# A new issue order on four engines, and one square read from PSUM, in the recurrent stage of a decoder

## The reference

```
h    = layer_norm(x) * ln1_w;  prev = h shifted by one token
k    = (h * mix_k + prev * (1 - mix_k)) @ Wk        # v and r likewise; r goes through a sigmoid
scan over t:  out_t   = (e1 * num + e2 * v) / (e1 * den + e2)   # running maximum kept in mx
              num,den = e1' * num + e2' * v , e1' * den + e2'
x    = x + (r * out) @ Wo
h    = layer_norm(x) * ln2_w;  prev = h shifted by one token
kk   = (h * cmix_k + prev * (1 - cmix_k)) @ Wck      # 128 -> 512 features
vv   = square(relu(kk)) @ Wcv                        # 512 -> 128
rr   = sigmoid((h * cmix_r + prev * (1 - cmix_r)) @ Wcr)
x    = x + rr * vv
```

## Time and profile before

| | |
|---|---|
| median of 3 runs | 4856.62 us |
| the profiled execution, its span | 4856.43 us, 4854.6 us |
| the recurrent stage in the span | first DMA issue at 1861.12, last instruction ends at 3038.0 |
| PE / DVE / ACT / POOL busy over the span | 90% / 73% / 65% / 38% |
| mean granted TensorE clock over the span | 0.963 of full speed |

### The profile page before, as it was taken

How to read it: one execution, slowest core, us unless ns; L and a number is a source line. 1 busy time by engine, 2 the same in 40 slices (tenths; PEclk the granted TensorE clock), 3 DMA queues, 4 the chain that set the end, 5 groups by cost and what they waited for, 6 DMA issues and landing times. The chain is left out here.

```text
span 4854.6 us, 101446 instructions
## 1 busy us (share of the span) xinstructions
PE 4353.9 (90%) x37343; PEld 2843.6 (59%) x37343; DVE 3537.1 (73%) x5307; ACT 3133.0 (65%) x5627; POOL 1846.5 (38%) x2204
## 2 busy tenths in 40 slices
PE   8989788889979987999999999779979989999888
PEld 6767556657757763333333333566657767777665
DVE  7978777567763338999999996663349966666748
ACT  6878677567764346888888888663247854444356
POOL 4444345014407751333333331037734422222327
PEclk9999899899989998999999999889999999999999
DMA  3000000000021122000000000411130000000110
GB/s 105 2 2 3 2 1 1 1 13 3 3 65 53 52 79 67 1 1 1 1 1 0 1 0 1 120 35 53 52 106 3 3 1 2 2 2 1 56 55 36
DMA packets 123884, 119.28 MB, mean 25 GB/s; under 512 B 19472, under 2 KB 103952, under 8 KB 122640
## 3 DMA queue, kind: packets, MB, share of 16 engines
q1 hardware_dynamic: 106000, 77.11, 5.1%
q0 software_dynamic: 17408, 35.69, 2.6%
HBM read 82.34 MB, written 30.41 MB: 23 GB/s over the span
## 5 line engine op out<-in xcount | busy, mean ns | idle before, releaser
L1759 POOL DMA_INDIRECT L_ffn_xg<-L_ffn_xrows,L_ffn_take x272 | 263.2, 968 | 280.6 <-DVE L_ffn_take L2054 198.4
L1823 PEld LDWEIGHTS L_ffn_ps<-L_ffn_early_down,L_ffn_mT 128*128 128x128 f32 x1904 | 248.3, 191 | 105.1 <-issue 78.0
L1765 POOL DMA_INDIRECT L_ffn_yrows<-L_ffn_yo,L_ffn_put x272 | 268.3, 987 | 100.4 <-issue 57.0
L2944 POOL TENSOR_TENSOR L_xattn_E<-L_xattn_E,L_xattn_rz 128x1024 f32<-128x1024 f32 x64 | 123.8, 1934 | 471.2 <-DVE L_xattn_rz L3164 471.2
L2247 PE MATMUL L_attn_ps<-L_attn_mix,L_attn_wck 128*128 128x512 f32 x512 | 246.3, 603 | 50.4 <-DVE L_attn_xw L2640 50.4
L2452 POOL TENSOR_TENSOR L_attn_dn<-L_attn_ex,L_attn_den 128x504 f32<-128x504 f32 x64 | 80.9, 1264 | 519.3 <-issue 424.7
L1803 PE MATMUL L_ffn_ps<-L_ffn_up,L_ffn_xT 128*128 x544 | 258.6, 557 | 18.9 <-DVE L_ffn_xT L2091 7.6
L1823 PE MATMUL L_ffn_ps<-L_ffn_early_down,L_ffn_mT 128*128 x1904 | 259.5, 276 | 2.5 <-DVE L_ffn_yo L2084 1.3
L2262 PE MATMUL L_attn_ps<-L_attn_rl,L_attn_wcv 128*128 128x512 f32 x512 | 246.3, 604 | 6.7
L1913 ACT ACTIVATE L_ffn_mT<-L_ffn_ps 128x512 f32<-128x512 f32 x136 | 81.2, 597 | 236.6 <-PE L_ffn_ps L1812 236.6
L2398 ACT ACTIVATE L_attn_rl<-L_attn_ps 128x1024 f32<-128x1024 f32 x128 | 129.8, 1014 | 160.5 <-PE L_attn_ps L2247 160.5
(11 more groups left out here) (619 smaller groups left out, 13458.1 us busy)
## 6 DMA issues: line engine op xcount, KB each, us to landing
L_ffn_row_hot<-L_ffn_yrows SPq DMA_DIRECT2D x32, 256.0 KB, 3.0
L_ffn_col_hot<-L_ffn_yrows SPq DMA_DIRECT2D x32, 256.0 KB, 3.4
L_ffn_w<-in_L_ffn_e_W SPq DMA_DIRECT2D x32, 256.0 KB, 4.3
L_ffn_xrows<-L_ffn_xtok SPq DMA_DIRECT2D x42, 192.0 KB, 2.1
L_ffn_xg<-L_ffn_xrows,L_ffn_take POOLq DMA_INDIRECT x272, 2.5
L_ffn_yrows<-L_ffn_yo,L_ffn_put POOLq DMA_INDIRECT x272, 2.3
main_x<-in_xT SPq DMA_DIRECT2D x8, 512.0 KB, 8.0
main_ctx<-in_ctxT SPq DMA_DIRECT2D x4, 1024.0 KB, 11.5
```

The costliest lines, as they stand in the source:

```text
L1759: pool.indirect_dma_start(xg[t % RING][:], None, xrows, bass.IndirectOffsetOnAxis(ap=take[:, t:t + 1], axis=0)) \
L1765: pool.indirect_dma_start(yrows, bass.IndirectOffsetOnAxis(ap=put[:, t:t + 1], axis=0), yo[t % RING][:], None).then_inc(scattered[t % RING ...
L1823: g = pe.matmul(ps[1][:, 3, 0:P], mT[u][0:rows[a], a * P:(a + 1) * P], down[a][:, bass.ds(at, P)], start=(a == 0), stop=(a == FT - 1))
```

## The change

The second half's square takes one operand from another place: `rl * rl`, both from SBUF, becomes `rl * kk`, the rectified value times the value still in PSUM (the product is the same number, since the rectified value is either that value or zero). PSUM banks 5 and 6 are therefore read until that product is done, and `hidden(m, 0)` of the next turn, which writes them, waits for it (`srb`). All four engines get a new order, by new places; VectorE's `prepare` steps get one too. No instruction is added or removed.

```diff
                 elif m:
                     pe.wait_ge(xc3, m)
+                    pe.wait_ge(srb, m)
...
 # TensorE
-                            (1.7, variance1), (22.9, keys), (24.9, values), (30.2, receptance), (45.7, output),
-                            (50.5, variance2), (60.6, lambda m: hidden(m, 0)), (59.9, receptance2),
-                            (63.9, lambda m: hidden(m, 1)), (69.8, lambda m: contract(m, 0)),
-                            (71.3, lambda m: contract(m, 1)), (76.0, centred))),
-                        (TURNS, NT, END, END_PERIOD, ((5.1, variance1), (16.3, end_sum), (21.4, end_variance2))))
+                            (1.6, variance1), (24.4, keys), (26.8, values), (32.6, receptance), (45.5, output),
+                            (50.4, variance2), (62.5, lambda m: hidden(m, 0)), (60.3, receptance2),
+                            (66.3, lambda m: hidden(m, 1)), (71.1, lambda m: contract(m, 0)),
+                            (71.2, lambda m: contract(m, 1)), (77.2, centred))),
+                        (TURNS, NT, END, END_PERIOD, ((6.3, variance1), (17.8, end_sum), (21.5, end_variance2))))
...
 # ScalarE
-                            (-12.9, square1), (13.0, half_mixed_r), (8.4, half_mixed_k), (-4.3, rstd1), (28.2, exp_r), (29.6, ln_r),
-                            (28.0, ln_denominator), (19.4, exp_ab), (21.0, exp_g), (34.5, reciprocal),
-                            (39.0, square2), (42.3, rstd2), (47.0, half_mixed), (46.9, half_mixed_r2), (53.5, lambda m: rectified(m, 0)), (55.0, squared),
-                            (57.0, lambda m: rectified(m, 1)),
-                            (55.4, exp_rr), (58.0, ln_rr), (63.6, sigmoid_rr))),
-                        (TURNS, NT, END, END_PERIOD, ((-9.3, square1), (-0.1, rstd1), (8.6, end_square2), (15.7, end_rstd2))))
+                            (-24.4, square1), (10.7, half_mixed_r), (6.6, half_mixed_k), (-3.5, rstd1), (25.7, exp_r), (27.4, ln_r),
+                            (28.2, ln_denominator), (17.3, exp_ab), (17.0, exp_g), (31.8, reciprocal),
+                            (37.2, square2), (40.3, rstd2), (44.3, half_mixed), (42.7, half_mixed_r2), (52.3, lambda m: rectified(m, 0)), (55.6, squared),
+                            (55.8, lambda m: rectified(m, 1)),
+                            (57.0, exp_rr), (59.6, ln_rr), (60.1, sigmoid_rr))),
+                        (TURNS, NT, END, END_PERIOD, ((-10.7, square1), (-1.6, rstd1), (7.8, end_square2), (13.2, end_rstd2))))
...
 # GpSimd
-            staggered(TURNS, PERIOD, (13.8, denominator), (20.8, denominator_r), (26.5, quotient), (36.1, normal2))
+            staggered(TURNS, PERIOD, (17.6, denominator), (21.7, denominator_r), (32.9, quotient), (38.8, normal2))
...
 # VectorE
-                dve.tensor_tensor(rl[:, 2:4, :], rl[:, 2:4, :], rl[:, 2:4, :], ALU.mult).then_inc(srb, 1)
+                dve.tensor_tensor(rl[:, 2:4, :], rl[:, 2:4, :], ps[:, 5:7, :], ALU.mult).then_inc(srb, 1)
...
-                            (8.8, normal1), (23.1, mix_r), (18.7, mix_key), (34.7, clamp_r), (23.4, running_max), (26.3, exponents_ab),
-                            (26.4, exponent_g), (27.1, clamp_g), (28.7, weighted), (28.0, scan_den), (34.2, scan_num),
-                            (29.2, bonus), (34.9, numerator), (45.5, residual1), (57.9, mix_k), (56.8, mix_r2), (68.0, squared),
-                            (61.1, clamp_rr),
-                            (70.9, gated), (76.6, residual2))),
-                        (1, NL - 1, PERIOD, PERIOD, ((2.7, prepare),)),
-                        (TURNS, NT, END, END_PERIOD, ((10.9, normal1), (28.1, end_close))))
+                            (13.0, normal1), (21.7, mix_r), (14.9, mix_key), (31.4, clamp_r), (21.4, running_max), (24.1, exponents_ab),
+                            (22.4, exponent_g), (22.8, clamp_g), (29.2, weighted), (29.2, scan_den), (29.3, scan_num),
+                            (31.1, bonus), (32.0, numerator), (46.5, residual1), (53.1, mix_k), (51.3, mix_r2), (65.6, squared), 
+                            (63.2, clamp_rr),
+                            (68.4, gated), (72.4, residual2))),
+                        (1, NL - 1, PERIOD, PERIOD, ((-16.9, prepare),)),
+                        (TURNS, NT, END, END_PERIOD, ((9.8, normal1), (26.1, end_close))))
```

## The result

The changed kernel takes 4739.27 us (median of 4 runs, 4733.29 to 4746.61) against 4855.57 us for the kernel before on the same chip: a ratio of 0.9762, 95% interval 0.9745 to 0.9779, 116.3 us less. The forecast was 4738 us. The profiled execution took 4733.29 us (span 4731.5), 6 us under its own median.

The account below looks back on a forecast made before the run. VectorE, never resting, was taken as the bound: 17.16 us a turn less 2.40, plus 0.26, 0.12 and 0.06, gives 15.20. Over 62 turns 121.5 us less, 3 lost at the ends: 118.5 less, 4738 us, range 4708 to 4798.

Parts of the forecast that it names:

- The mechanism: GpSimd's four instructions each need about 1.07 us in which VectorE runs no instruction with two SBUF operands; first starter wins.
- One sign: GpSimd's `denominator` and `normal2` were to become longer than before, held by a scan and by `normal1`.
- `clamp_g` shut out: VectorE's `clamp_g` would be shut out by GpSimd's `quotient`, adding 0.26 us a turn (bounds 0 and 0.4).
- `clamp_g` behind its own input: VectorE's `clamp_g` directly behind `exponent_g`: 0.77 us start to start against 0.65 back to back, adding 0.12 a turn.
- The two handovers: `denominator` against `normal1` and `normal2` against `numerator` have no slack: 0.06 us a turn added (bounds 0 and 0.3).
- The new wait and the PSUM operand: TensorE's `hidden(m, 0)` waiting on the square costs nothing; the square from PSUM takes 1.22 us, gaining 0.16 a turn.
- TensorE next: TensorE's 34 matmuls a turn at 0.43 us make 14.6 us; no order goes below about 14.9 a turn.
- The ends: First and last turns: `prepare(1)` waiting for weights and a later `normal1(1)`, partly returned; 3 us lost (4 gained to 9 lost).
- The step that failed: VectorE never rests in the old kernel, so its order and 21 instruction lengths set the 17.16 us period.
- four separate gains: VectorE's lost waits per turn: `mix_k` 1.02, `mix_r` 0.79, `numerator` 0.43, the square 0.16; together 2.40 us.
- Rival 4: The square stays shut out despite its PSUM operand: 0.16 us a turn, 4748 us; chance inside the forecast's 0.55.
- the rival that was meant to be the slow one: GpSimd's `denominator_r` misses its gap, delaying ScalarE's `exp_ab`: period 17.9 us, time 4905 us; chance 0.05.

## Why the prediction was right, and where it was not

*The mechanism, right.* GpSimd and VectorE shut each other out, and the new order sets GpSimd's four instructions beside VectorE's PSUM operations. On the prediction's clock (0 at `normal1`, 2402.07), `numerator` was due at 1.8 and came at 1.80, `mix_k` 4.3 and 4.32, `running_max` 5.55 and 5.58, `mix_r` 6.7 and 6.71, `clamp_g` 8.1 and 8.12, `exponents_ab` 8.7 and 8.77. The four went to the lengths of the earlier trace rows. The Trainium skill says the same of who waits ("SBUF — State Buffer", "Who interferes with whom": two SBUF inputs on VectorE contend with a GpSimd instruction that reads SBUF, the one that issues second blocks until the first is done). The rows here agree, with tails of 0.54 for a 512-wide instruction. One sign was wrong: `normal2` was to be longer than before and is shorter, 1.35 after 1.89, since `scan_num` had held it in the old order and `normal1` holds it for less.

*What came back, right in place, a little off in size.* `clamp_g` shut out: 0.31 measured, 0.26 forecast. `clamp_g` behind its own input: 0.77 from start to start, 0.12 as forecast. The two handovers cost nothing (0.06 forecast). Period 15.17 against 15.20.

*The new wait and the PSUM operand cost nothing, right.* The square ends at 2402.16; the `hidden(m, 0)` that waits for it starts at 2407.88, 5.7 us later, after the end of `residual2` and right behind TensorE's own `receptance2`. The square takes 1.20 with one operand from PSUM, and 1.22 with both from SBUF. The Trainium skill ("VectorE: DVE Perf Modes", section on the TRN2 errata) gives a fixed part of 120 cycles for an operation from PSUM against 58 from SBUF; 62 cycles are 0.065 us, an estimate from that page. The square, with one operand of each kind, shows no such difference.

*TensorE next, right in size.* 34 matmuls at 0.43 are 14.6 of the 15.17; the kernels in which no VectorE instruction is shut out run at 14.89 to 14.92, forecast 14.85 to 14.95. The prediction's chain from `gated` to `residual1` is the one that the rows show, though it closes through VectorE. TensorE's busy share was forecast at 96% and is 99.85%, with 0.22 us free at one place: this share says little here.

*The ends, wrong in sign.* The forecast had 3 more turns' gain less 3 us (bound 9), so 2.9 gained. Measured from the stage's first DMA issue (1861.12 before, 1858.97 after) the fill lost 11.9: `normal1(4)` came 61.0 us after it before and 72.9 after. The drain, from `normal1(63)` to the stage's last instruction, gained 5.8 (103.5 against 97.7). `prepare(1)` waiting for its weights is 4.0 of the loss at `normal1(0)` (8.4 and 12.4 us after the first issue), a little over the 1.5 to 3.6 that the prediction's bounds allow; giving it back returned 3.3. The other 7.9 us lie between the next `normal1` rows: 12.6 us from turn 0 to turn 1 instead of 7.6, 14.9 from turn 1 to turn 2 instead of 12.1, and the next two together alike to 0.1. The first is the idle stretch that the prediction named for `normal1(1)`, behind all of turn 0's scans; it comes with VectorE's order (12.6 in the kernel that has this order alone, 7.7 in the one that has the others alone). Together the ends lost 6.1 us, in the forecast's terms a loss of 12.0 where 3 was taken. Stage in all: 59 x 1.99 = 117.6 less, 11.9 more, 5.8 less, so 111.4 less. The profiled executions differ by 123.1; the other 11.7 lie outside the stage, in code that is the same. What follows the stage took 1807.0 us in this execution, 1816.6 before, and 1811.8 to 1821.1 in the profiles of the eleven experiments: run to run, as this execution's distance from its median. 4738 against 4739.27 is therefore closer than the parts deserve, and partly luck: the ends cost 9 us more than forecast, each turn saved 0.03 more (1.9 us in 59), so the stage fell 7 us short of the 118.5, and the spread outside it, between executions of the same code, gave 5 of them back.

*The step that failed.* "VectorE never rests in a turn; its order and the length of its 21 instructions are the period", and with it the addition of four separate gains. The old period was a circle over ScalarE, GpSimd, the shut-out `mix_r` and VectorE's way to `exp_ab`; the time of `mix_r` that looked busy was slack: it gave up 0.33 to the added instruction and took in the 0.18 that the square lost, and the period stayed. `mix_k`'s 1.02, taken away by the other engines' orders alone, brought 0.38. The square's 0.16 a turn is worth 0.00 in the old order and 2.89 in the new one (18.06 less 15.17). Rival 4 priced a square still shut out at 4748; that kernel runs at 4918, past even the rival that was meant to be the slow one. The sum came out because it counts VectorE's instructions without the time shut out, in the new order, and that needs no knowledge of what bound the old one; with all four out of GpSimd's way VectorE's sum is the period, as the added instruction shows, and it was counted rightly.

## What to carry to other kernels

An engine that is 100% busy is not yet the bound: look whether its long instructions end a fixed time after another engine's, and follow that other engine back; if the path returns to the same instruction a turn later, it is a circle, and time taken off an instruction that has slack against it gains nothing. Test it by adding a small instruction: free ahead of `mix_r` before, 1:1 ahead of the square after. The answer holds for the place where the instruction stands. Where GpSimd must work beside VectorE, give it the stretches in which VectorE has a PSUM operand, and check every handover, since one collision shifts the engine into the next.

## What the runs showed of the hardware

- Shutting out works both ways and whole: a 512-wide VectorE instruction ends 0.54 us after GpSimd's, a 1024-wide one 1.08 after; GpSimd's ends 1.06 to 1.14 after VectorE's.
- GpSimd gets in between two VectorE instructions that stand back to back: in the kernel with the square from SBUF, `denominator` waited through `scan_num`, and the square right behind lost, not GpSimd.
- One SBUF operand is no protection in itself: `clamp_g` (SBUF to SBUF) was shut out, 0.72 against 0.41, while products with one SBUF and one PSUM operand never were in the middle of the stage (0.65 to 0.69 for 512 columns, in both kernels and with the square from SBUF). `clamp_g` is also the step that takes its columns fastest, 0.41 for 504 where `clamp_r` from PSUM takes 0.66 for 512; whether that is why, no run here tests.
- The profile counts the time shut out as busy, on both engines: GpSimd's `denominator` shows 2040 ns on the mean over 64 turns in the profile's group of that line, 1264 before, with the kernel faster:

```profile
L2453 POOL TENSOR_TENSOR L_attn_dn<-L_attn_ex,L_attn_den 128x504 f32<-128x504 f32 x64 | 130.5, 2040 | 385.4 <-issue 293.0
```
